# A hybrid attention and expert kernel: gates spread by DMA, an opening with four banks, and a second attention that turns q once

## The reference

```python
x = x + attn_a(layernorm(x))   # 16 heads of 8, q and k rms-normed, softmax, output projection with bias
x = x + ffn(layernorm(x))      # 8 experts, top 2 by softmax(x @ gate_w.T), and one shared expert
x = x + attn_b(layernorm(x))   # 16 heads of 8 with rotary tables; pairs of heads subtracted with a factor
x = x + ffn(layernorm(x))      # the same weights again
# expert e, for all tokens: xe = x * gate[e]; h = silu(xe @ w1[e]) * (xe @ w3[e]); out += h @ w2[e]
```

## Time and profile before

| | us |
|---|---|
| median of 3 runs | 990.37 (986.24 to 992.31) |
| the profiled execution | 989.17 |
| its span, first to last instruction | 987.4 |
| TensorE busy | 874.8 (89%) |
| VectorE busy | 732.5 (74%) |
| ScalarE busy | 578.9 (59%) |
| GpSimd busy | 528.6 (54%) |
| mean granted TensorE clock | 0.973 of full speed |

### The profile page before, as it was taken

One profiled execution on the slowest core, in us unless ns is written; L12 is line 12 of the kernel. 1 busy time (PEld: TensorE's weight loads), 2 busy tenths in 40 slices (PEclk: granted clock), 3 DMA queues, 4 the chain that ended last, 5 costly groups with the idle time before them and its releaser, 6 DMA issues.

```text
span 987.4 us, 22246 instructions
## 1 busy us (share of the span) xinstructions
PE 874.8 (89%) x7264; PEld 621.0 (63%) x7264; DVE 732.5 (74%) x1978; ACT 578.9 (59%) x903; POOL 528.6 (54%) x610
## 2 busy tenths in 40 slices
PE   2799999888999999999788888888878799999998
PEld 0355555545688777788555555555545688888887
DVE  4677777766777777777678898989883577767775
ACT  1478778766444434444488888888875344444443
POOL 4666666663444455554436575757542644454551
PEclk9999999988999999999899999999997899999999
DMA  8000000000000000000000000000000000000000
GB/s 235 1 2 1 0 0 0 0 2 2 1 1 1 1 1 0 0 1 1 1 2 1 1 0 0 0 0 0 1 1 1 1 12 12 12 7 4 11 11 23
DMA packets 14607, 8.70 MB, mean 9 GB/s; under 512 B 1616, under 2 KB 14160, under 8 KB 14544
## 3 DMA queue, kind: packets, MB, share of 16 engines
q1 hardware_dynamic: 12960, 7.28, 2.6%
q10 hardware_dynamic: 1584, 0.62, 0.2%
HBM read 5.80 MB, written 2.10 MB: 8 GB/s over the span
## 4 chain that ended last, share of the span: by engine, by line
PE 21%; issue 13%; DVE 11%; POOL 7%; ACT 2%; DVEq 0%; POOLq 0%; ACTq 0%
DVE s_qs L1088 6%; PE psum L819 5%; PE psum L787 5%; POOL f_xe_lo L1434 3%; POOL f_p L1444 3%; PE psum L1327 2%; PE psum L769 2%; PE psum L1289 1%; DVE f_xe L1471 1%; PE psum L885 1%; PE psum L1291 1%; PE psum L1290 1%; PE psum L874 1%; PE psum L804 1%; ACT f_xe_hi L1403 1%
## 5 line engine op out<-in xcount | busy, mean ns | idle before, releaser
L1403 ACT ACTIVATE f_xe_hi<-f_xe 128x512 fp32r<-128x512 f32 x128 | 80.9, 632 | 204.6 <-DVE f_xe L1471 204.6
L1434 POOL TENSOR_TENSOR f_xe_lo<-f_xe,f_xe_hi 128x512 fp32r<-128x512 f32 x64 | 83.9, 1311 | 184.6 <-ACT f_xe_hi L1403 184.6
L1088 DVE TENSOR_REDUCE s_qs<-psum 128x4 fp32r<-128x1024 f32 x128 | 156.3, 1222 | 35.4 <-PE psum L804 34.6
L1327 PEld LDWEIGHTS psum<-w,f_h 128*128 128x128 f32 x1152 | 147.7, 191 | 8.8
L1327 PE MATMUL psum<-w,f_h 128*128 128x128 f32 x1152 | 153.0, 276 | 0.0
L467 ACT ACTIVATE s_probs<-psum 128x1024 f32<-128x1024 f32 x128 | 125.9, 1023 | 33.1 <-PE psum L354 32.7
L955 ACT ACTIVATE s_probs<-psum 128x1024 f32<-128x1024 f32 x128 | 131.3, 1026 | 19.5 <-PE psum L787 17.8
L1289 PE MATMUL psum<-f_xe_hi,w_hi 128*128 128x512 f32 x288 | 127.0, 441 | 7.6 <-POOL f_xe_lo L1434 7.0
L1487 DVE TENSOR_TENSOR f_h<-psum,f_g 128x512 f32<-128x512 f32 x144 | 99.2, 689 | 44.9 <-ACT f_g L1388 34.6
L1291 PE MATMUL psum<-f_xe_lo,w_hi 128*128 128x512 f32 x288 | 114.1, 396 | 0.0
L1290 PE MATMUL psum<-f_xe_hi,w_lo 128*128 128x512 f32 x288 | 113.5, 394 | 0.0
(11 more groups left out here) (177 smaller groups left out, 1732.6 us busy)
## 6 DMA issues: line engine op xcount, KB each, us to landing
out<-x SPq DMA_DIRECT2D x8, 256.0 KB, 2.3
x<-in_x SPq DMA_DIRECT2D x3, 512.0 KB, 9.6
w<-in_w SPq DMA_DIRECT2D x3, 512.0 KB, 7.5
x<-in_x SPq DMA_DIRECT2D x2, 256.0 KB, 3.9
select_raw<-in_select SPq DMA_DIRECT2D x1, 512.0 KB, 4.8
rope_cos<-in_rope_cos SPq DMA_DIRECT2D x1, 256.0 KB, 3.9
rope_sin<-in_rope_sin SPq DMA_DIRECT2D x1, 256.0 KB, 4.6
wqkv_a<-in_Wqkv_aT ACTq DMA_DIRECT2D x1, 192.0 KB, 3.6
```

The costliest lines, as they stand in the source:

```text
L1088: dve.tensor_reduce(o[:, r:r + 2, 2 * p:2 * p + 2, 24:25].bitcast(F32R), room(km, i).rearrange("p (r j s) -> p r j s", r=2, j=2), AX.X, AL ...
L1327: ins = pe.matmul(Y[k % 2][:, t * P:(t + 1) * P], g.f_h[:, q, t * P:(t + 1) * P], g.w2[:, e, :], start=(e == 0 and t == 0), stop=(e == NE ...
L1434: pool.tensor_tensor(xe_lo[:, ring(e), :], src, xe_hi[:, ring(e), :], ALU.subtract).then_inc(xe_lo_pool.sem, 1)
```

## The change

The gates: VectorE transposes the gates of a chunk in blocks of 32, SP writes them to DRAM (`gates`) and reads them back for one expert at a time, the same row for all 128 partitions, into four places `gt`. The matmul with `select`, its loads and casts, the turn of the gates on TensorE and its eviction are gone. `scale` multiplies `gt` by xt. The low parts: experts 2 and 3 on VectorE, the other seven on GpSimd, the shared expert's in slot 2 of its own chunk between those of 5 and 6. Normalisation, turn, gate matmul, `best`, masks and powers run one chunk earlier than before, at other slots; the statistics have their own slot.

The opening: x in eight parts of which four wait for the first weights; the projections of the first two sequences in two banks and the four turns of the first in four; the Newton steps of the first sequence on VectorE; parts of the second sequence's preparation earlier; an activation that loads ScalarE's table early. In the first attention the splits of the expert weights stand at steps 5 and 11.

The second attention: q is turned once into `s_qt`; the reduce writes into a small tile, which TensorE turns and ScalarE evicts as 16 rows, and a DMA puts them into row 24 of each group of `s_qt` (two per sequence). Two small VectorE ops (L1139, L1164) become GpSimd additions, with a factor moved into wo. Turns and tokens stand at other steps.

```diff
-PARTS = ((0, 4), (4, 8), (8, 16), (16, 24), (24, 32))
-STATISTICS = ((-3, 0), (-2, 11), (-1, 12), (0, 8), (0, 12))
-ROOTS = ((-3, 0), (-2, 15), (-1, 15), (0, 15), (1, 5))
+PARTS = tuple((t, t + 4) for t in range(0, NT, 4))
+LOADED = ((0, 1), (1, 1), (2, 2), (2, 2), (3, 4), (3, 4), (3, 4), (3, 4))
+STATISTICS = {(-3, 0): (0,), (-3, 12): (1,), (-1, 8): (2,), (-1, 12): (3,), (0, 4): (4,), (0, 11): (5,), (1, 4): (6,), (1, 9): (7,)}
+ROOTS = {(-3, 0): (0,), (-2, 5): (1,), (-1, 13): (2, 3), (0, 14): (4, 5), (1, 14): (6, 7)}
...
         for i, (lo, hi) in enumerate(PARTS):
-            sp.dma_start(g.x[:, lo:hi, :], x_view[:, lo:hi, :]).then_inc(x_loaded[i], 16)
+            if i == 4:
+                sp.wait_ge(first_loaded, first_count)
+            sp.dma_start(g.x[:, lo:hi, :], x_view[:, lo:hi, :]).then_inc(x_loaded[LOADED[i][0]], 16)
...
+                act.wait_ge(filled, 1)
+                act.activation(tiny[:, 60:61], g.minus_half[:, 0:1], ACT.Exp)
...
-            if (k, h) == (-3, 0):
+            for i in STATISTICS.get((k, h), ()):
+                statistics(i)
+            if (k, h) == (-2, 2):
...
+NEWTON_ON_DVE = 1
+EARLY_A = {(1, "norm", 0): (-3, 11), (1, "xt", 0): (-2, 5), (1, "xt_keep", 0): (-2, 8), (1, "qkv", 0): (-2, 9),
+           (1, "qkv", 1): (-2, 10), (1, "square", 0): (-2, 12), (1, "sums", 0): (-1, 3), (1, "newton", 0): (-1, 4)}
...
+    def room(m, c):
+        return bank(3) if m < 2 and c == 1 else XB
+    def turned(m, i):
+        return bank((5, 0, 1, 2)[i]) if m == 0 else QK
...
-                else:
+                elif km > 0:
                     pe.wait_ge(qp_sb.sem, qp_sb.upto(m, 1))
-                turn(QK, ks[:, km % 2, c]).then_inc(kt_mm.sem, 1)
+                turn(turned(km, 2 * c), ks[:, km % 2, c]).then_inc(kt_mm.sem, 1)
...
+                if k in (13, 14) and h == 5:
+                    pool.wait_ge(w_hi_sb.sem, k - 12)
+                    w, hi, lo = ((g.w1, g.w1_hi, g.w1_lo), (g.w3, g.w3_hi, g.w3_lo))[k - 13]
+                    pool.tensor_tensor(lo[:], w[:], hi[:], ALU.subtract)
...
+                if km < NEWTON_ON_DVE:
+                    dve.wait_ge(seed.sem, seed.upto(m))
+                    i = 0
+                    for o, u, w, op in newton_steps():
+                        if i:
+                            dve.wait_ge(newton.sem, newton.upto(m, i))
+                        dve.tensor_tensor(o[:], u[:], w[:], op).then_inc(newton.sem, 1)
+                        i += 1
...
-            if k == 12:
-                dve.wait_ge(g.late_loaded, g.late_count)
-                dve.tensor_copy(g.w1_hi[:], g.w1[:]).then_inc(w_hi_sb.sem, 1)
-                dve.tensor_copy(g.w3_hi[:], g.w3[:]).then_inc(w_hi_sb.sem, 1)
-                dve.tensor_copy(g.select[:], g.select_raw[:])
             for h in part:
+                if k in (12, 13) and h == 11:
+                    dve.wait_ge(g.late_loaded, g.late_count)
+                    if k == 12:
+                        dve.tensor_scalar(g.wo[:], g.wo[:], 4 * (1.0 - LAMBDA_INIT), None, ALU.mult)
+                    w, hi = ((g.w1, g.w1_hi), (g.w3, g.w3_hi))[k - 12]
+                    dve.tensor_copy(hi[:], w[:]).then_inc(w_hi_sb.sem, 1)
...
-    "kt": (8, 19), "qp": (11, 16), "max": tuple(range(14, 30, 2)), "qf": (7, 15), "v": (4,),
-    "otr": (2, 4), "tokens": (2, 4), "diff": (6,), "sq2": (6,), "mean": (7,), "pow": (8,), "head": (8,), "atr": (12,),
+    "kt": (7, 19), "qp": (11, 15), "max": tuple(range(14, 30, 2)), "mt": (8, 16), "v": (4,),
+    "otr": (3, 5), "tokens": (3, 5), "diff": (6,), "sq2": (6,), "mean": (7,), "pow": (8,), "head": (8,), "atr": (13,),
     "pj": (14,), "residual": (15,), "stats": (11, 13), "rstd": (14,),
 }
...
-                    ins = pe.matmul(room(km, i)[:, o:o + SEQ], qp[r:r + 24, q, c * P:(c + 1) * P],
+                    ins = pe.matmul(room(km, i)[:, o:o + SEQ], qt[r:r + 24, km % 2, q, c * P:(c + 1) * P],
...
+            def max_turn(m, km, p):
...
+                pe.transpose(QK[0:16, 0:P], mxs[:, km % 2, p].rearrange("p r j c -> p (r j c)"),
+                             g.identity[:]).then_inc(mt_mm.sem, 1)
...
+                        act.wait_ge(row_sb[p].sem, row_sb[p].upto(m - 1))
+                        act.activation(mt[0:16, p, :], QK[0:16, 0:P], ACT.Copy).then_inc(mt_sb.sem, 1)
...
+                    pool.wait_ge(ms_sb.sem, ms_sb.upto(m))
+                    pool.tensor_tensor(g.s_var2[:], g.s_ms2[:], g.rms_eps[:], ALU.add).then_inc(var_sb.sem, 1)
...
+                    pool.wait_ge(mv_sb.sem, mv_sb.upto(m))
+                    pool.tensor_tensor(g.s_vare[:], g.s_mv[:, 0:2, 1], g.ln_eps[:], ALU.add).then_inc(vare_sb.sem, 1)
...
-                dve.tensor_reduce(o[:, r:r + 2, 2 * p:2 * p + 2, 24:25].bitcast(F32R),
+                dve.tensor_reduce(mxs[:, km % 2, p, r:r + 2, :, c:c + 1].bitcast(F32R),
...
-                dve.tensor_scalar(g.s_vare[:], g.s_mv[:, 0:2, 1], LN_EPS, None, ALU.add).then_inc(vare_sb.sem, 1)
...
+    def sync(sp):
+        for m in range(NSEQ):
+            n = Step(None, 0, m)
+            for p in range(2):
+                sp.wait_ge(mt_sb.sem, mt_sb.upto(n, p + 1))
+                sp.dma_start(qt[24:P:32, m % 2, 2 * p:2 * p + 2, :].rearrange("r j (c t) -> r (j c) t", c=2).bitcast(F32),
+                             mt[0:16, p, :].bitcast(F32)).then_inc(row_sb[p].sem, 16)
...
-LOW_ON_DVE = (2, 5, 6, 7)
+LOW_ON_DVE = (2, 3)
+LOW_ON_POOL = (0, 1, 4, 5, 8, 6, 7)
...
-LEAD = {1: (0,), 3: (1,), 4: (2,), 6: (3,), 8: (4,), 9: (5,), 13: (6,), 15: (7,)}
+LEAD = {0: (0,), 2: (1,), 3: (2,), 5: (3,), 6: (4,), 7: (5,), 13: (6,), 15: (7,)}
...
 FF = {
-    "norm": 8, "x_turn": 0, "xt_sb": 0, "logits": 1, "best": 1, "pow": (2, 2, 2, 2), "gates": 5, "s_turn": 6,
-    "st_sb": 6, "residual": 0, "rstd": 0,
+    "norm": 4, "x_turn": 5, "xt_sb": 5, "logits": 6, "best": 7, "masks": 8, "pow": 7, "sums": 2, "gates": 3,
+    "residual": 5, "stats": 6, "rstd": 8, "shared": 2,
 }
-FF_LEAD = {"x_turn": 0, "xt_sb": 1, "logits": 2, "best": 2, "exp": 4, "gates": 5, "s_turn": 6, "st_sb": 6}
+FF_LEAD = {"x_turn": 0, "xt_sb": 1, "logits": 2, "best": 2, "masks": 2, "exp": 4, "sums": 5, "gates": 5}
...
+    def turned(n, k, e, task):
+        return ([(n + 1, k + 1)] if k == -1 and e == FF_LEAD[task] else []) + (
+            [(n + 2, k + 2)] if k + 2 < NCH and e == FF[task] else [])
...
+    def inputs(n, k, e):
+        return [x for x in ahead(n, k, e, 3) if x[2] < E] + ([(n, k, E)] if e == FF["shared"] and 0 <= k < NCH else [])
...
-            def spread(m, km, e):
...
-                pe.matmul(SB, g.select[:, e, :], st[:, km % 2, :],
-                          start=True, stop=True).then_inc(sb_mm.sem, 1)
...
-            def s_turn():
-                pe.wait_ge(lo_sb.sem, lo_sb.upto(n + 1))
-                for t in range(4):
-                    ins = pe.transpose(T[:, t * P:(t + 1) * P], ssp[:, t, :], g.identity[:])
-                ins.then_inc(st_mm.sem, 1)
...
+                if e == FF["pow"] and k + 2 < NCH:
+                    pool.wait_ge(sh_sb.sem, sh_sb.upto(n + 2))
+                    w = 4 * E // PIECES
+                    for i in range(PIECES):
...
-                dve.wait_ge(sb_mm.sem, sb_mm.upto(m, e + 1))
+                dve.wait_ge(xt_sb.sem, xt_sb.upto(m))
+                dve.wait_ge(gt_sb[e % 4].sem, gt_sb[e % 4].upto(m, 16 * (e // 4 + 1)))
...
-                dve.tensor_tensor(xe[:, e % 2, :], SB, xt[:, km % 2, :], ALU.mult).then_inc(xe_sb.sem, 1)
+                dve.tensor_tensor(xe[:, e % 2, :], gt[:, e % 4, :], xt[:, km % 2, :], ALU.mult).then_inc(xe_sb.sem, 1)
...
+                dve.tensor_tensor(g.f_m[:, 0, :, :].rearrange("p t e -> p (t e)").rearrange("p (e t) -> p t e", t=4),
+                                             g.f_m[:, 1, :, :],
                                              bc(g.f_rs[:].unsqueeze(2), [P, 4, E]), ALU.mult).then_inc(sc_sb.sem, 1)
-                dve.wait_ge(sc_sb.sem, sc_sb.upto(n + 1))
-                dve.wait_ge(st_mm.sem, st_mm.upto(n))
-                dve.tensor_copy(ssp[:, :, 0:E].bitcast(F32R), g.f_m[:, 0, :, :]).then_inc(hi_sb.sem, 1)
...
+        def store(m):
+            view = out.rearrange("(n s) (c p) d -> n p (s c) d", s=2, p=P)
+            sp.wait_ge(x_sb.sem, x_sb.upto(Step(None, 0, m)))
+            sp.dma_start(view[m], g.x[:, 4 * m:4 * m + 4, :]).then_inc(stored, 16)
+        for m in range(NCH):
+            n = Step(None, 0, m)
+            sp.wait_ge(sg_sb.sem, sg_sb.upto(n))
+            sp.dma_start(g.gates[m % 2].rearrange("e (t b j) -> b (e t) j", t=4, b=4),
+                         g.f_sg[:]).then_inc(written.sem, 16)
+            sp.wait_ge(written.sem, written.upto(n))
+            for e in range(E):
+                if e >= 4 or m > 0:
+                    sp.wait_ge(xe_sb.sem, xe_sb.upto(n, e - 3) if e >= 4 else xe_sb.upto(n - 1, e + 5))
```

(9 more changed lines are left out.)

302 lines of the change are left out of this document (136 added, 166 removed).

## The result

The changed kernel takes 984.13 us (median of 20 runs, 978.04 to 987.49), the kernel before 988.78 in the same comparison (20 runs). The ratio is 0.9948, 95% interval 0.9933 to 0.9962: 5 us faster, where 16 were forecast. The median lies inside the forecast range, but the gain is a third of the forecast one. The profiled execution has a span of 984.8 against 987.4; with 986.6 us it is the second slowest of the 20, so that its trace shows 2.6 us of the 5. Medians can include single disturbed executions of the slower state, which the ratios leave out.

A forecast was written before the change was run, and what follows sets the result against it. It took TensorE and a four-engine chain before each slot to bound the feed-forwards, and VectorE the second attention. Terms +9 - 5 - 8.5 - 12.5 + 1 = -16 took 989.2 to 973.2, forecast as 974, range 946 to 1001.

The forecast's parts named there:

- Feed-forward chunks, +9: Both feed-forwards: the scale, now with both inputs in SBUF, waits for GpSimd's low part; 9 us slower in all.
- Scales up to 1.9 long: Sign in the feed-forwards: scales lasting up to 1.9 us instead of 0.68, with chunks near 27.5.
- the 26.0: Feed-forward chunk time if no scale waits for GpSimd: slots of 2.55 to 2.6 plus the normalisation; -14 in all.
- rival (c): Feed-forwards: GpSimd's powers lock VectorE too, scales and low parts 2 and 3 wait; +48, 1022 us; chance 0.03.
- rival (a): Feed-forwards: the scale does not wait for GpSimd; -14 instead of +9, 951 us; chance 0.15.
- Splits -5: First attention: expert weight splits moved to steps where they no longer lock VectorE's cast; -5 us, bounds -7 and 0.
- opening -8.5: Start to first scores: Newton steps on VectorE, more banks, smaller statistics groups; -8.5 us, bounds -12 and -4.
- Second attention, -12.5: Second attention: a sequence falls from 16.9 to 16.0 us, times 14; -12.5, bounds +4 and -27.
- Transitions, +1: Between layers: the first chunk's gates come two steps earlier but travel 6.2 us; +1 us.
- (b), late gates: Scale 0 of every chunk waits for two DMA transfers taking 10.6 us; +52, 1026 us; chance 0.10.
- the slack of 7.8: Feed-forward chunk: 7.8 us from the end of gates to scale 0, hiding 6.2 us of DMA travel.
- (d), no gain in the second attention: Second attention: the later tokens take what VectorE gives, so nothing is gained; 986 us; chance 0.14.

The follow-up runs named there:

- xt_psum: Changed kernel, with ScalarE copying the turned input once a chunk into a free PSUM bank where the scale reads it; 971.9 us, ratio 0.9841.
- small_on_dve: Changed kernel with the second attention's two small additions back on VectorE; one execution, nine steady sequences take 153.6 us against 144.7.
- new_b: Kernel before with only the second attention, its tables and sync queue from the changed one; 985.7 us, ratio 0.9954.
- old_ff: Changed kernel with the feed-forwards, their tables and the loads of select from the kernel before; 973.9 us, ratio 0.9875.
- lead_exp: Changed kernel with chunk 1's powers taken by ScalarE's exponential instead of GpSimd; 986.0 us, ratio 0.9968.
- lead_old: Changed kernel with the slots ahead of the first chunk at the steps of the kernel before; 984.1 us, ratio 0.9945.
- light1: Changed kernel with three quarters of chunk 1's preparation left out in both feed-forwards' leads, so its gates are wrong; 975.6 us, ratio 0.9875.
- warm_x: xt_psum plus matmuls nobody reads before waits in the passages, but not before the first experts' matmuls; 963.5 us, ratio 0.9746.
- newton_pool: Changed kernel with the Newton steps of sequence 0 on GpSimd again; one execution, first exponentials at 31.5 us against 30.5.
- new_a: Kernel before with only the opening, first attention and their tables from the changed one; 978.8 us, ratio 0.9917.
- best: best_cold plus matmuls nobody reads ahead of TensorE's waits in the passages; 974.9 us, ratio 0.9844.
- best_cold: Changed kernel with the scale's turned input in PSUM and the slots ahead of the first chunk spread over two sequences; 971.4 us, ratio 0.9801.

## Why the prediction was wrong, point by point

The sum inside the layers came out nearly as forecast, in part because misses cancel. The term that failed is the last and smallest, the transitions.

**Feed-forward chunks, +9: right in mechanism and nearly in size.** Scales up to 1.9 long were to show it, and they reach 1.51. In the table's stretches +4.8 came of +5.7. From scale 3 to 4 a chunk took 2.59 as worked out, and from scale 7 to the next scale 0 5.11 against 5.1; from 6 to 7 it was 4.4 to 4.7, not 5.2. The pieces that the working names for that step (0.68, 1.3, 1.4, 0.8 and 0.6) add up to 4.8 and not to 5.2. xt_psum shows the cause by taking it away. Its full chunks of 26.6 and 26.4 stand above the 26.0 that was the bound without the wait. The Trainium skill ("SBUF — State Buffer", "SBUF: two separate sides") says that a VectorE op with two SBUF inputs and a GpSimd op that reads SBUF hold the shared ports against each other. The 34 long scales agree, the 40 beside the powers do not: those read SBUF too, 8 columns at a time, and held nothing. Here the measurement decides. That was rival (c), and it fell; rival (a) fell with the first lengthened scale.

**Splits -5 and opening -8.5: the sum right, by luck.** Together -13.7 against -13.5, as one gave 2 us more and the other 2 less. The splits gave 7.1 (45.1 to 38.0 from sequence 12 to 15), the lower end of their bounds. The casts no longer meet GpSimd's work:

```profile
199.59 0.43 DVE L602 CAST s_ks<-s_qh 128x512 fp32r<-128x512 f32 x1 [0.21 <-POOL s_qh L559]
...
202.27 2.65 POOL L529 TENSOR_TENSOR w_lo<-w,w_hi 128x1152 fp32r<-128x1152 f32 x1
```

The opening gave 6.3 at the fourth sequence, which starts at 73.4 in this trace; in other executions of the same opening it starts from 70.9 on, those without a stretch at the lower clock near 55 us. The first scores come at 29.70, not near 28 (before: the earlier trace rows). The Newton steps on VectorE end at 17.6 instead of 22.4, but the product behind them waits for the scale vector, and starts at 18.41:

```profile
17.43 0.22 DVE L628 TENSOR_TENSOR s_y<-s_y,s_yt 128x64 f32<-128x64 f32 x1
17.57 0.17 DVE L233 TENSOR_TENSOR open_tiny<-lam_in 128x16 f32<-128x16 f32 x1
...
18.41 1.07 POOL L555 TENSOR_TENSOR s_qh<-s_qkv,s_y 128x512 f32<-128x512 f32 x1 [7.81 <-DVE qk_scale L239]
```

From there to the first scores are 11.3 us, where the working had 8.8: that is the mis-sized piece. The second sequence's preparation was moved ahead of the first scores, where it stands in the same queues; that this is the reason no run shows.

**Second attention, -12.5: the size of a sequence right, its parts and the count wrong.** 16.9 became 16.1, where 16.0 was forecast. But small_on_dve gives all of it to the two small VectorE ops (0.9 to 1.0 a sequence, where I had 0.55 for one and less for the other), and so nothing to the second turn of q: VectorE leads there with 89%, and what leaves TensorE and ScalarE is not on the path. And the gain ends where VectorE ends to be the bound: it is at 89% in the window of ten sequences and at 79% in the 17.3 us of sequence 13, as the preparation of later ones runs out, and sequence 15 has no maxima at all. From sequence 12 to 15 the 51.7 became 52.1, and 51.3 to 51.5 in new_b, old_ff, lead_exp, lead_old and light1. I multiplied by 14 what holds for 12 at most: -8.2 instead of -10.8 in the table's stretch, and nothing of the -1.8 behind it.

**Transitions, +1: the step that failed.** They cost 12 more than forecast: +14.6 came in the three passages of the traces for +2.5. The working saw one thing, the gates' travel, took 6.2 for it where the traces show 5.1 to 6.1, and set against it "two steps earlier". The steps did come earlier in the code, but the last product of the gates starts 11.9 us after the last sequence's first exponentials, in old_ff 10.6: chunk 1's normalisation (1.1) had been put between. What it left out:
- The work that the change moves into the passage. I took 4 us for its leaving chunk 6 and charged nothing where it went. light1 takes three quarters of it away: 7 us by the ratios, a part of it by the clock.
- The granted clock. warm_x shortens the passages by adding work: 8 to 9 us for 44 us less at the lower level. And in the changed kernel itself an execution with more time at the lower level is a longer one, by 0.15 us for each us of it (a straight line through the 20; correlation 0.73); between its trace and that of newton_pool it is 0.22 in the third passage and 0.24 in the middle one. The three passages together had 38 us more at the lower level than before. My estimate from these prices is that the clock makes 6 to 9 of the 14.6.
- The clock is not all of it. old_ff is 7 us faster than the changed kernel by the ratios, and its four executions spent 90 us at the lower level in the mean, as much as the changed kernel's 87. light1 is 7 us faster for 13 us less, which at the same prices is 2 to 3. These causes overlap, as waits and low clock come together in the passages, so their prices don't add up to the 12.
- What unchanged code loses. The third passage of new_a has nothing of the change in it and is 5.4 longer than before, that of old_ff and new_b 3.2 and 3.4, each with 34 to 38 us at the lower level instead of 20 (one execution of each). A gain ahead of such a stretch is not kept by itself.

By its sentence on the clock in the splits' term the prediction knew the mechanism, and used it only where the change took a stall away. The Trainium skill ("TensorE: Matmul & The Clock Gate", "HAM oscillation — how this bites in real kernels") says that waits between short bursts of matmuls throw the engine back to the lower level again and again, and that this costs time of its own; warm_x against xt_psum agrees, with 8 to 9 us.

**Rivals.** (b), late gates, holds only in the third passage (4.44 once), never in a chunk: scale 0 waits for no DMA there, so the slack of 7.8 was enough (there the first row landed 1.3 us or more before it). (d), no gain in the second attention, is nearest in time (986) but for another reason. What stays open is how the 14.6 of the passages split between moved work, gates and clock: the runs that took one away changed the clock too, and this varies between executions of one kernel (0.946 to 0.967 in the 20 of the changed one), so that one trace of each can't settle it.

## What to carry to other kernels

Cut both traces at the same instructions before believing a sum: inside the layers this one was right to 1.5 us in sum, and the miss lay in the passages, which a steady-state working does not see. Work that is moved a stage earlier has to be charged where it lands, above all in the short stretch ahead of a loop, and a stretch in which TensorE already waits can pay twice, by the wait and by the clock. One trace of such a stretch is not enough: the same instructions took 104.5 and 110.6. An operand moved from PSUM to SBUF can cost more than the matmuls it saves: here a copy of 0.6 us a chunk back into a free bank gave 11 us.

## What the runs showed of the hardware

- A VectorE op of 512 columns with both inputs in SBUF took 1.17 instead of 0.68 us beside a GpSimd op of 512 columns (34 cases), and 0.68 beside GpSimd's powers of 8 columns (40 cases). With one input in PSUM, in xt_psum, it was never longer than 0.689 (128 cases).
- The small ops had the same: L1543, 32 columns,

```profile
L1543 DVE TENSOR_TENSOR f_sh<-f_lg,f_top x16: 172/942/957, 231.9 to 932.3; 128x32 f32<-128x32 f32 x16
```

  took 0.94 in the 14 cases beside a low part.
- A transpose of 32 columns in blocks on VectorE took 0.21. A store of 16 KB to DRAM and a wait for it took 2.04 between the two issues (235.77 to 237.81), and a row of 2 KB read back into all 128 partitions 3.3 in the median. From the end of the transpose to the landing of the first row were 5.1 to 6.1.
- Matmuls without a reader brought TensorE's granted clock from 0.956 to 0.977 (xt_psum against warm_x, medians) and gained 8 to 9 us where they stood in waits. With some ahead of the first experts' matmuls too, in a kernel with earlier slots, they cost 3.5 us (best against best_cold).
- The same instructions of the changed kernel's third passage took 110.6 us in one execution, with 44 us of it at the lower TensorE level, and 104.5 in one of newton_pool, with 17.
